# Graph network layers: SyncE fetches 19 of 980 chunks of node rows, one row to a DMA

## The reference

```
# layer 0, twice:  h = h @ W ;  out[dst] += h[src] * norm ;  + b
# layer 1:  z = xc[src]                                # xc: h, normed in 8 capsules of 16 features
#           three times:  p = softmax(einsum(z, u[dst])) ; u = l2norm(segment_sum(z * p, dst) + xc)
# layer 2:  mean of h[src] over the edges of each dst ;  relu(. @ W + b)
# layer 3:  segment_sum(gelu([h[src], edge_attr] @ W1 + b1) @ W2 + b2, dst) ;  layernorm with gamma and beta
```

## Time and profile before

| what | value |
|---|---|
| median of three runs | 6136.25 us |
| span of the profiled execution | 6133.4 us |
| GpSimd busy (POOL) | 4562.7 us, 74% |
| TensorE busy (PE) | 3912.3 us, 64% |
| VectorE busy (DVE) | 3726.0 us, 61% |
| ScalarE busy (ACT) | 1638.9 us, 27% |
| DMA, mean over the span | 114 GB/s |

### The profile page before, as it was taken

The page is one execution under the profiler, slowest core; times in us unless marked ns, Lnnn a source line. Parts: engine busy times, 40 slices in busy tenths (PEclk is TensorE's granted clock), DMA queues, the critical chain, the costliest instruction groups (busy, mean ns, idle before and its releaser), DMA issues. The chain is left out here.

```text
span 6133.4 us, 123500 instructions
## 1 busy us (share of the span) xinstructions
PE 3912.3 (64%) x27584; PEld 3400.1 (55%) x27585; DVE 3726.0 (61%) x9157; ACT 1638.9 (27%) x4058; POOL 4562.7 (74%) x5214
## 2 busy tenths in 40 slices
PE   1555555555555477777789989956566665666665
PEld 1544444455455366666578878845555553555553
DVE  6333333565666677777887787775555555555555
ACT  1000000112121333333455565531111113222222
POOL 6777777677777677777778888857777776777776
PEclk9666666666666688888899999977777776888887
DMA  4222222222222355555577777732222222222222
GB/s 124 68 70 68 70 69 68 62 69 68 70 68 70 103 175 171 172 170 171 169 231 248 249 226 248 249 109 69 69 69 69 70 68 54 71 71 71 69 71 95
DMA packets 447304, 697.73 MB, mean 114 GB/s; under 512 B 89485, under 2 KB 204570, under 8 KB 446282
## 3 DMA queue, kind: packets, MB, share of 16 engines
q0 software_dynamic: 127616, 263.32, 16.6%
q10 hardware_dynamic: 210816, 255.92, 12.8%
q1 hardware_dynamic: 108746, 177.24, 9.1%
HBM read 506.58 MB, written 189.53 MB: 113 GB/s over the span
## 5 line engine op out<-in xcount | busy, mean ns | idle before, releaser
L759 POOL DMA_INDIRECT u_parts<-table,src x3128 | 2951.6, 944 | 1063.2 <-issue 952.1
L835 PE MATMUL ps_sum<-u_parts,onehot 128*128 x2928 | 655.5, 395 | 691.6 <-SPq L588 552.2
L1374 DVE SCALAR_TENSOR_TENSOR onehot<-dst,minus_row,beside 128x512 f32<-128x512 f32 x1100 | 816.9, 744 | 365.7 <-issue 308.6
L835 PEld LDWEIGHTS ps_sum<-u_parts,onehot 128*128 128x128 f32 x2928 | 573.7, 291 | 776.2 <-issue 775.4
L759 POOL DMA_INDIRECT ring<-table,src x782 | 746.2, 954 | 264.9 <-issue 237.7
L835 PE MATMUL ps_u<-u_parts,onehot 128*128 x2928 | 535.9, 343 | 515.6 <-SPq L588 452.2
L835 PEld LDWEIGHTS ps_sum<-msg,onehot 128*128 128x128 f32 x4896 | 693.7, 213 | 306.8 <-issue 149.1
L835 PE MATMUL ps_sum<-msg,onehot 128*128 128x128 f32 x4896 | 753.9, 303 | 127.0 <-DVE msg L457 96.9
L835 PEld LDWEIGHTS ps_u<-u_parts,onehot 128*128 128x128 f32 x2928 | 473.0, 246 | 566.0 <-issue 565.0
L1669 DVE TENSOR_TENSOR zu<-ps_u,ring 128x512 f32<-128x512 f32 x732 | 502.7, 687 | 351.7 <-SPq L588 192.6
L885 PE MATMUL ps_u<-u_parts,hots 128*128 x5856 | 487.9, 235 | 56.2 <-ACT hots L1144 39.4
(11 more groups left out here) (205 smaller groups left out, 6477.8 us busy)
## 6 DMA issues: line engine op xcount, KB each, us to landing
ring<-z_rows SPq DMA_DIRECT2D x392, 256.0 KB, 3.5
hot_rows<-hots ACTq DMA_DIRECT2D x244, 256.0 KB
hots<-hot_rows ACTq DMA_DIRECT2D x244, 256.0 KB, 3.4
z_rows<-ring SPq DMA_DIRECT2D x196, 256.0 KB, 2.1
u_parts<-table,src POOLq DMA_INDIRECT x3128, 2.5
table<-hots ACTq DMA_DIRECT2D x122, 256.0 KB
wide<-hot_rows ACTq DMA_DIRECT2D x122, 256.0 KB, 3.4
wide_t<-hot_rows ACTq DMA_DIRECT2D x122, 256.0 KB, 3.5
```

Of the source, the lines that this page charges most:

```text
L759: nc.gpsimd.indirect_dma_start(out=slot(p, c % slots)[:, t * P:(t + 1) * P], out_offset=None, in_=tables[p], in_offset=bass.IndirectOffset ...
L835: last = nc.tensor.matmul(sums[k % len(sums)][:, 0:P], lhsT=(onehot[:, k % HOTS, :, :] if hots_of is None else hots_of)[:, t, :], rhs=rows ...
L1374: V.scalar_tensor_tensor(out=buffers[k % len(buffers)], in0=per_row(dst[:, ds(chunk * TILES, TILES)], [P, TILES, P]), scalar=minus_row0[:, ...
```

## The change

In each gather pass some chunks are no longer gathered by GpSimd: four in each of the passes with 14 slots (chunks 55, 101, 148 and 194) and three in CAPS1 (68, 131 and 194). These follow from `rows_by` and `staged_chunks` in the diff. GpSimd skips them.

SyncE fetches their rows instead, while it attends to the other chunks. The numbers of the rows, `staged`, are loaded at the start into partition 0 of SBUF, and VectorE shifts them left by 9 once, so that each is the byte offset of a row in the table. The four-chunk list lies in a part of `ring` that is free in CONV1 and CONV2, and is kept in HBM (`row_offsets`) over the capsule passes; the three-chunk list lies in `attr`. At chunk position c of a pass SyncE issues the DMAs of the next rows. There are 2048 rows over 186 positions, 11.01 for each, in the passes with 14 slots, and 1536 rows over 189 positions, 8.13 for each, in CAPS1. Each is one `dma_start` of 512 bytes from the table in HBM to its place in `far_rows` (in CAPS1: in `z_rows`), also in HBM, seen as bytes and so cut in 16 pieces of 32 bytes. The offsets are loaded into registers for two positions at a time (`LISTS`). When a staged chunk's turn nears, SyncE waits for its 512 rows and moves the 256 KB to their slot with one DMA. The staged chunks of CAPS1 are in `z_rows` already and are not saved again.

SyncE's gather passes are written out for all 196 positions in place of a loop over rounds; the waits are on the same events as before. As a tile of a DMA on GpSimd now is 128 edges in a row, the host lays out `src`, `dst` and `attr` in another order of the edges inside a chunk.

```diff
+ROW_CHUNKS = {p: 4 if SLOTS[p] == FAR else 3 for p in GATHERS}
+BACK = {p: RING if SLOTS[p] == FAR else LAG for p in GATHERS}
+def load_position(p, c):
+    return c - SLOTS[p] + BACK[p]
+LISTS = 2
+LAST_FETCH = {p: load_position(p, CHUNKS - 2) - 1 for p in GATHERS}
+def rows_by(p, c):
+    return min(ROW_CHUNKS[p] * CHUNK, (c + 1) * ROW_CHUNKS[p] * CHUNK // LAST_FETCH[p])
+def staged_chunks(p):
+    done = [next(c for c in range(CHUNKS) if rows_by(p, c) >= CHUNK * (k + 1)) for k in range(ROW_CHUNKS[p])]
+    return [next(c for c in range(CHUNKS) if load_position(p, c) > at + 1) for at in done]
...
+            sp.wait_ge(list_scaled, 2)
+            sp.dma_start(row_offsets, far_list).then_inc(list_copied, 16)
...
+                def offsets_of(r0, r1, p=p):
+                    return nc.values_load_multi_w_load_instructions(
+                        row_lists[p][0:1, ds(r0, r1 - r0)], engines=[ENGINE.SP], ...)[1]
+                def fetch_rows(r0, offsets, p=p):
+                    table = tables[p].bitcast(u8).rearrange("n f -> (n f)")
+                    for r, offset in enumerate(offsets, r0):
+                        k, e = divmod(r, CHUNK)
+                        t, row = divmod(e, P)
+                        place = row_place(k).bitcast(u8)[row, t * ROW_BYTES:(t + 1) * ROW_BYTES]
+                        sp.dma_start(place.unsqueeze(0), table[ds(offset, ROW_BYTES)].unsqueeze(0)).then_inc(rows_staged[...][k], 16)
+                def gathered(p=p):
+                    back = BACK[p]
+                    for c in range(CHUNKS):
+                        if c % RING == 0:
+                            keys = ((keys[RING:] if len(keys) > RING else keys) if c else ())
+                            keys = tuple(keys) + tuple(keys_of(c, RING))
...
+                        if c in STAGED[p]:
+                            sp.wait_ge(staged_in_slot, 16 * staged_by(p, c))
                         else:
-                            publish(j, q, last)
+                            sp.wait_ge(rows_in[c % SLOTS[p]], landed_by(p, c))
+                        sp.sem_inc(landed, 1)
+                        if p == CAPS1 and c not in STAGED[p]:
+                            sp.dma_start(z_rows[c], ring[:, c % RING, :]).then_inc(z_saved[c % RING], 16)
+                        old = c - back
+                        if old >= 0:
                             if p == CAPS1:
+                                sp.wait_ge(z_saved[old % RING], saved_by(old))
+                            free(keys[old - (c // RING * RING - (len(keys) - RING))])
+                        for k, d in enumerate(STAGED[p]):
+                            if c == load_position(p, d):
+                                sp.wait_ge(rows_staged[GATHERS.index(p) % 2][k], fetched_by(p, k))
+                                sp.dma_start(slot(p, d % SLOTS[p]), row_place(k)).then_inc(staged_in_slot, 16)
+                        r0, r1 = (rows_by(p, c - 1) if c else 0), rows_by(p, c)
+                        if c % LISTS == 0:
+                            r_list = r0
+                            r_end = rows_by(p, c + LISTS - 1)
+                            offsets = offsets_of(r0, r_end) if r_end > r0 else ()
+                        fetch_rows(r0, offsets[r0 - r_list:r1 - r_list])
...
@@ gpsimd
                 for c in range(CHUNKS):
+                    if c in STAGED[p]:
+                        continue
                     if c >= slots:
                         pool.wait_ge(slot_free, before_this + c + 1 - slots)
-                    for t in range(TILES if c < CHUNKS - 1 else LAST_TILES):
+                    for t in range(tiles_of(c)):
@@ vector
+            dve.wait_ge(list_loaded, 32)
+            for listed in (far_list, caps_list):
+                V.tensor_scalar(listed, listed, ROW_SHIFT, None, ALU.logical_shift_left).then_inc(list_scaled, 1)
```

More of the change, by code:

```diff
@@ L14 @@
 DST_ROW = CHUNK // 2
+ROW_BYTES = P * 4
+ROW_SHIFT = 9
+assert ROW_BYTES == 1 << ROW_SHIFT
 DST_ROWS = CHUNKS * CHUNK // DST_ROW
@@ L216, in build @@
         z_saved = [sem(f"z_saved{j}") for j in range(RING)]
-        z_seen = sem("z_seen")
+        list_loaded = sem("list_loaded")
+        staged_in_slot = sem("staged_in_slot")
+        list_scaled = sem("list_scaled")
+        list_copied = sem("list_copied")
+        rows_staged = [[sem(f"rows_staged{i}_{k}") for k in range(ROW_CHUNKS[CONV1])] for i in range(2)]
         landed = sem("landed")
@@ L576, in _, with publish_loaded, free @@
                           .then_inc(h_in[q], 16)
[L577 to L587, removed]
+                def publish_loaded(j, q, p=p):
+                    sp.wait_ge(rows_loaded[j], (q + 1 + uses_before(p, j, (CAPS2, CAPS3))) * 16)
                     sp.sem_inc(landed, 1)
[L590 to L594, removed]
+                def free(key, p=p):
                     sp.wait_ge(msg_ready if p in (CAPS1, CAPS2, CAPS3) else step_summed,
@@ L602, in keys_of @@
                         max_val=STEPS - 1, skip_runtime_bounds_check_because=BY_TABLE)[1]
[L604 to L619, removed]
@@ L621, in round_of, with loaded_round @@
-                def round_of(q, first, last=False, p=p, loads=loads):
+                def loaded_round(q, first, p=p):
                     c0 = q * RING
-                    keys = () if first and loads else keys_of(c0 if first else c0 - RING, RING if first else 2 * RING)
-                    at = 0 if first else RING
+                    keys = () if first else keys_of(c0 - RING, 2 * RING)
                     for j in range(RING):
                         back = j - LAG
[L628 to L638, removed]
-                        else:
-                            publish(j, q, last)
-                            if p == CAPS1:
[L642 to L654, removed]
+                        if not first or back >= 0:
+                            publish_loaded(back % RING, q if back >= 0 else q - 1)
@@ new lines, in loaded_round @@
+                        if not first:
+                            free(keys[j])
+                        elif p == CAPS3:
+                            free(keys_left[j], p - 1)
+                        elif j >= RING - LAG:
+                            sp.wait_ge(z_saved[j], saved_by(CHUNKS - RING + j))
+                            free(keys_left[j], p - 1)
+                        sp.dma_start(ring[:, j, :], z_rows[ds(c0 + j, 1), :, :]
+                                     .rearrange("c p n -> (c p) n")).then_inc(rows_loaded[j], 16)
@@ L655, in _ @@
                 if loads:
+                    loaded_round(0, True)
+                    with sp.Fori(1, CHUNKS // RING) as q:
+                        loaded_round(q, False)
                     for j in range(RING - LAG, RING):
[L657 to L660, removed]
+                        publish_loaded(j, CHUNKS // RING - 1)
@@ new lines, in _ @@
+                    keys_left = keys_of(CHUNKS - RING, RING)
+                else:
+                    if p in (CONV1, MEAN):
+                        sp.wait_ge(table_stored, 16 * len(CUTS) * (1 if p == CONV1 else 2))
+                    else:
+                        sp.wait_ge(rows_stored, 16 * WINDOWS * ((CONV2, CAPS1, EDGE).index(p) + 1))
+                    if p == CONV1:
+                        sp.wait_ge(list_copied, 16)
+                    if p == MEAN:
+                        sp.dma_start(far_list, row_offsets).then_inc(list_copied, 16)
+                        for half in range(FAR // RING):
+                            load_attr(half, half)
+                        sp.wait_ge(list_copied, 32)
+                    keys_left = gathered()
@@ L662, in _ @@
+                if p not in (CAPS1, CAPS2):
+                    for j in range(0 if loads else RING - BACK[p], RING):
+                        free(keys_left[j])
             sp.wait_ge(rows_stored, 16 * WINDOWS * 4)
```

54 lines of the change are left out of this document (45 added, 9 removed).

## The result

The changed kernel takes 9970.97 us (median of four runs, 9969.14 to 9971.94), the kernel before beside it 6135.82. The ratio is 1.625, with the 95% interval [1.6227, 1.6273]. It is slower, as forecast, but by 3835 us where 1829 were forecast, and above the range.

What follows compares the result with a forecast made beforehand. GpSimd bounds the kernel before; with the rows SyncE becomes the bound. Four 14-slot passes add 1616 us and CAPS1 213 to 6133.4 of span, 7965 us with 2.9 around it; range for 8 in 10: 6600 to 8500.

Steps and rivals of the forecast that it cites:

- What bounds the kernel before, and where the bound moves: Gather passes: GpSimd bounds before at 4.99 us a chunk; after, SyncE at 7.28 us a position against GpSimd's 4.89.
- The issue of a row: SyncE's row DMA: 333 ns an issue, bounds 270 and 391; a whole row 0.442 us, bounds 0.31 and 0.50.
- dearer rows: Rival on SyncE's rows and lists: 391 ns an issue and 0.247 us a number throughout, 8783 us; chance 0.05.
- The MOVE: SyncE's register instruction for a row's offset: one of 29 ns a row, bounds 0 and 1.
- rival 2: SyncE's rows: no MOVE, or row DMAs as cheap as L543's 270 ns; 7294 us; chance 0.13.
- The lists: SyncE's register loads of row offsets: 363 us a 14-slot pass, 1.95 a position; CAPS1 317 us, 1.67 a position.
- Rival 3: SyncE's list loads: fast for every start, 0.71 us a position in place of 1.95; 6845 us; chance 0.11.
- The old work and CAPS1: SyncE's existing work: 0.46 us a position in 14-slot passes, 0.93 in CAPS1, where a position totals 6.19 us, pass +213.
- The removed gathers: GpSimd loses 4 x 16 gathers at 1.248 us and 12 at 1.258 us, together 95 us.
- The skill's rule: Skill page: issue time is usually small relative to the DMA, so SyncE's part would be small and the first rival come.
- the first rival: All of it fits: row with its list under 0.40 us (CAPS1 0.49), GpSimd stays the bound, 6041 us; chance 0.14.

Runs made afterwards that it cites:

- p1_prices: Changed kernel with another kind of row DMA in four passes; in CONV1 the source address is constant and the lists are not loaded; 9299.0 us.
- aligned: Changed kernel with `rows_by` rounded down so that every list load begins at a multiple of four numbers; 8877.75 us, ratio 1.447 to the kernel before.
- norows: Changed kernel without row DMAs and list loads, staged chunks filled from the table's first rows by one DMA each; 6056.54 us, ratio 0.987 to the kernel before.
- direct2: Changed kernel with rows of the 14-slot passes sent into SBUF in one piece, each chunk then copied to its slot; 7595.99 us, ratio 1.2373.

## Why the prediction was wrong

**What bounds the kernel before, and where the bound moves.** Right. GpSimd waited for nobody; after, it waits 4097 us for SyncE, and SyncE for landings 39.

**The issue of a row: the step that failed.** "No copy from HBM to HBM is in the trace. Bounds 270 and 391 ns; I take 333." All lines that I read have one end in SBUF, and I took the shape (16 pieces, all engines) for what prices an issue, and the kind of copy for nothing. With one end in SBUF 16 pieces are 369 to 420 ns, near my number; between two HBM ends they are 538. The bounds were drawn from rows of the other kind, so the true value lay outside them, and even the rival "dearer rows" fell short (8783 us). A row is 0.635 us in place of 0.442: 9728 x 0.193 = 1.88 ms of the 2.01 ms by which I missed. Some 0.09 ms more lie outside the passes, where my sum had nothing: from the last gather of a pass to the next pass 52 us before CAPS1 and 61 before EDGE, where it was 28 and 33, and 80 us after the last gather of all, where it was 52. I had written that no such copy is in the trace and drew no consequence from it; it was the reason to leave the range open above.

**The MOVE.** Right in number, wrong in price. It was 0.069 us of my 0.442; the pass without it, CONV1 of p1_prices, has the same beat. The part of rival 2 that leaves out the MOVE would have brought nothing here.

**The lists.** Right: 1742 us for my 1769 (4 x 363 + 317), and aligned, the reverse, gave back what the loads shrank by. Rival 3 (all fast) was not the case as built and is a line of code away; it had priced the lists at 1769 - 922 - 198 = 649 us, and aligned has 646.

**The old work and CAPS1.** 0.46 us holds: CONV2 by my own sum with the measured row is 186 x (11.01 x 0.635 + 1.90 + 0.46) + 26 = 1765 us, and 1765 was measured. In CAPS1 the save is dearer behind a row, 0.15 us on the mean, which I had not seen: 189 x (8.13 x 0.637 + 1.72 + 0.93 + 0.15) + 27 = 1535, measured 1528.

**The removed gathers.** 76 are worth 95 us of GpSimd, but even where they are all that is left some 12 us are lost outside the passes (norows).

**The skill's rule.** The Trainium skill, page "DMA: Bandwidth & Descriptors", section "Issuing engines are not separate DMA queues", has the issue as usually small relative to the DMA. By it the first rival would have come, 6041 us; the runs disagree for rows of 512 B. 9728 issues of 0.635 us are 6.2 ms of SyncE's 9.97, while the packets of its DMA queue, saves and loads included, took 7.3% of the 16 engines' span by the page of the profile. The measurement decides. How long a single row takes to land is in no view.

## What to carry to other kernels

Price a DMA's issue by a row of the same kind, and that means both its ends: where the trace has none between two HBM tensors, leave the range open above, or measure it first. Work put on an idle engine is free only while all of it, loads and issues, stays under that engine's idle time for each turn, with room to spare: here 4.4 us a position. Three chunks straight to SBUF fit; four filled the room so fully that the others got their chunks up to 30 us late; four from HBM to HBM did not fit at all. And when a part of a loss is a matter of alignment (the start of a register load), take that first; it was 1.1 ms here for one line.

## What the runs showed of the hardware that was not expected

- The issue of a DMA on SyncE depends on where its ends are: 228 ns for one piece of 512 B into SBUF, 369 for 16 pieces, 538 to 627 with both ends in HBM for 1 to 16 pieces.
- Between two HBM ends the first issue after a pause is shorter (median 492 for 538 ns, 468 for 589 with a constant source), and the beat of 0.62 us is the same with and without the MOVE: in a train of such DMAs it is not the instruction that sets the pace. Into SBUF the first issue is the longer one (263 for 228 ns, direct2).
- A DMA from SBUF right behind such a copy is held up too: in the changed kernel the issue of the 256 KB save has a median of 510 ns where it begins within 0.25 us of the end of a row's issue (158 of 193), and of 338 where it begins later.
- A register load from SBUF in the 14-slot passes costs 0.24 us for four numbers where it starts at a multiple of four (20 numbers 1.20 us, 24 numbers 1.42, aligned), and 0.20 us for each number where it doesn't: 22 numbers take 1.6 or 4.5 us in the changed kernel.
